# A decoder layer on one core: products of the high parts ahead of the low parts, a finer wait, and a new order on all five engines

## The reference, cut to what matters

```
h  = LN(x) * g + b, cut into 4 heads of 64
x1 = LN(x + (x + relu(h @ k.T)**2 @ v))         k, v = w_fc and w_proj.T as 1024 rows of 64, for all heads
Q, K, V = x1 @ Wq.T + bq, ctx @ Wk.T + bk, ctx @ Wv.T + bv                   (16 heads of 16)
D  = clip(frac_k - frac_q, -0.2, 0.2)
P  = softmax(gamma * Q @ K.T / 4 + delta * (alpha_pos * max(D, 0) + alpha_neg * min(D, 0)))
x2 = LN(x1 + (P @ V) @ Wo.T + bo)
e  = the largest of 8 of x2 @ gate_W.T + gate_b;   u = x2 @ lora_A[e].T       (rank 4)
f  = relu(x2 @ wi_W.T + wi_b + u @ lora_B[e].T)                               (1024 wide)
out = LN(x2 + f @ wo_W.T + wo_b)
```

## Time and profile before

| What | Value |
|---|---|
| median of 3 runs | 902.18 us (898.16 to 902.9) |
| the profiled execution's own time | 896.02 us |
| its span, from the first to the last instruction | 894.2 us |
| mean granted TensorE clock in it | 0.993 |
| TensorE busy, of the span | 839.8 us, 94% |
| VectorE, ScalarE, GpSimd busy | 760.4, 716.8, 587.9 us |

### The profile page before, as it was taken

The page is one execution under the profiler, slowest core; times in us unless marked ns, Lnnn a source line. Parts: engine busy times, 40 slices in busy tenths (PEclk is TensorE's granted clock), DMA queues, the critical chain, the costliest instruction groups (busy, mean ns, idle before and its releaser), DMA issues.

```text
span 894.2 us, 20601 instructions
## 1 busy us (share of the span) xinstructions
PE 839.8 (94%) x7012; PEld 667.6 (75%) x7012; DVE 760.4 (85%) x2158; ACT 716.8 (80%) x1949; POOL 587.9 (66%) x762
## 2 busy tenths in 40 slices
PE   2787989999999999999999999999999999999866
PEld 1354757878888787887877787788878787788766
DVE  4778889989898898989889898989889798899842
ACT  3568899888897988888897988889798888889821
POOL 2867776776767686776777586776768676544310
PEclk9999999999999999999999999999999999999998
DMA  6223323222132222223123222213222221313100
GB/s 173 86 51 55 65 38 62 38 46 41 43 67 58 43 49 54 43 56 58 43 42 72 37 43 54 54 43 50 64 42 48 50 49 24 77 22 53 31 12 23
DMA packets 40025, 46.12 MB, mean 52 GB/s; under 512 B 10257, under 2 KB 27153, under 8 KB 39922
## 3 DMA queue, kind: packets, MB, share of 16 engines
q1 hardware_dynamic: 39922, 44.82, 25.1%
HBM read 15.42 MB, written 4.19 MB: 22 GB/s over the span
## 4 chain that ended last, share of the span: by engine, by line
PE 87%; ACT 6%; DVE 3%; issue 2%; POOL 1%; POOLq 0%; DVEq 0%; ACTq 0%
PE bank L226 21%; PE bank L270 12%; PE bank L351 12%; PE bank L415 10%; PE bank L364 7%; PE bank L258 6%; PE bank L342 6%; PE bank L259 6%; ACT P L564 2%; PE bank L422 2%; PE bank L290 1%; ACT STG L489 1%; ACT R L510 1%; PE bank L376 1%; PE bank L247 1%
## 5 line engine op out<-in xcount | busy, mean ns | idle before, releaser
L988 POOL TENSOR_SCALAR U<-DP,alph 128x512 f32<-128x512 f32 x256 | 186.9, 731 | 128.4 <-DVE NM L778 72.6
L970 POOL TENSOR_TENSOR R<-R 128x512 f32<-128x512 f32 x212 | 228.0, 1076 | 64.2 <-ACT R L510 64.1
L564 ACT ACTIVATE P<-T,NM 128x256 f32<-128x256 f32 x512 | 256.3, 511 | 2.9 <-DVE NM L778 2.9
L771 DVE SCALAR_TENSOR_TENSOR bank<-DN,alph,bank 128x512 f32<-128x512 f32 x256 | 191.2, 747 | 40.8 <-PE bank L342 38.5
L778 DVE CUSTOM_DVE_ANT_0 T<-bank,U 128x256 f32<-128x256 f32 x512 | 197.0, 422 | 9.0 <-DVE bank L771 0.2
L510 ACT ACTIVATE R<-bank 128x512 f32<-128x512 f32 x256 | 152.6, 598 | 46.7 <-PE bank L259 42.3
L489 ACT ACTIVATE STG<-bank 128x512 f32<-128x512 f32 x256 | 152.4, 595 | 27.5 <-PE bank L351 25.7
L351 PE MATMUL bank<-ident,P 128*128 128x128 f32 x1024 | 155.5, 274 | 6.9 <-ACT STG L489 5.8
L351 PEld LDWEIGHTS bank<-ident,P 128*128 128x128 f32 x1024 | 117.5, 140 | 29.9 <-ACT P L564 14.7
L270 PE MATMUL bank<-R,VS 128*32 128x512 f32 x1024 | 124.1, 603 | 4.9 <-DVE R L727 3.9
L258 PE MATMUL bank<-SK,KH 128*128 128x512 f32 x256 | 115.5, 451 | 5.7 <-DVE SK L721 5.7
(11 more groups left out here) (164 smaller groups left out, 1887.7 us busy)
## 6 DMA issues: line engine op xcount, KB each, us to landing
QS<-QK SPq DMA_DIRECT2D x384, 64.0 KB, 2.3
XG<-in_x SPq DMA_DIRECT2D x16, 256.0 KB, 3.1
CT<-in_ctxT SPq DMA_DIRECT2D x16, 256.0 KB, 2.8
out<-XO SPq DMA_DIRECT2D x16, 256.0 KB, 2.5
FK<-in_frac SPq DMA_DIRECT2D x16, 128.0 KB, 3.2
STG<-in_wiT SPq DMA_DIRECT2D x2, 512.0 KB, 4.0
STG<-in_woT SPq DMA_DIRECT2D x2, 512.0 KB, 4.0
STG<-in_kT SPq DMA_DIRECT2D x2, 256.0 KB, 3.9
```

The lines of the kernel that those rows point to most:

```text
L564: eng.activation(P[n % NP][:, cs], T[n % NT][:, cs], ACT.Exp, bias=NM[:, n % 8, q:q + 1], scale=-1.0, accum_out=SU[n // 16 % 2][:, q, seat ...
L771: eng.scalar_tensor_tensor(out=L[:, :], in0=dn[:, :], scalar=alph[:, 16 + h:17 + h], in1=L[:, :], op0=ALU.mult, op1=ALU.add).then_inc(s_t1, 1)
L970: eng.tensor_tensor(r[:, :], r[:, :], r[:, :], ALU.mult).then_inc(s_sqp, 1)
L988: eng.tensor_scalar(U[n % NU][:, :], dp[:, :], alph[:, h:h + 1], 0.0, ALU.mult, ALU.add).then_inc(s_u, 1)
```

## The change

Four things. First, `kp`, `qp`, `vp`, `op` and `gate` run all products with the high part behind a wait for the high part alone, then wait for the low part and run its products. The number of matmuls stays the same (5986 instructions of that kind in both programs). Second, `ffn_out` waits per piece for the quarter that it reads. Third, the two low-rank matmuls become a step of their own, `low_rank`, with a place of its own in the order. Fourth, nearly all the numbers in `due` and the single instants are new on all engines, and with them the order.

```diff
             def kp(b):
...
-                pe.wait_ge(s_cl, b + 1)
+                pe.wait_ge(s_ch, b + 1)
                 wh, wl = W["k"]
                 for m in range(2):
                     cs = slice(m * 128, m * 128 + 128)
                     for k in range(2):
-                        mm3(bank[:, m * 256:m * 256 + 256], wh[:, k, cs], wl[:, k, cs], CH[:, k, :], CL[:, k, :],
-                            k == 0, k == 1, s_kp if m + k == 2 else None)
+                        for x in (wh, wl):
+                            eng.matmul(bank[:, m * 256:m * 256 + 256], x[:, k, cs], CH[:, k, :],
+                                       start=(m + k == 0 and x is wh), stop=False, skip_group_check=True)
+                pe.wait_ge(s_cl, b + 1)
+                for m in range(2):
+                    cs = slice(m * 128, m * 128 + 128)
+                    for k in range(2):
+                        i = eng.matmul(bank[:, m * 256:m * 256 + 256], wh[:, k, cs], CL[:, k, :], start=False,
+                                       stop=(k == 1), skip_group_check=True)
+                i.then_inc(s_kp, 1)
...
             def op(b):
-                pe.wait_ge(s_aol, b + 1)
-                by_tokens("op", b, "o", s_op)
+                by_tokens("op", b, "o", (s_aoh, b + 1), (s_aol, b + 1), s_op)
...
+
+            def low_rank(b, f2):
+                bank = bank_of["fi", b, f2]
                 pe.wait_ge(s_ull, b + 1)
...
-                    pe.wait_ge(s_il, 4 * b + 4)
                 bank = bank_of["fo", b, 0]
                 t = piece // 4
+                pe.wait_ge(s_il, 4 * b + piece % 4 + 1)
...
-                for b, u in due(g, 1327, 4, 22, early=-3, late=708):
+                for b, u in due(g, 1322, 4, 25, early=-1, late=761):
                     ffn_in(b, u)
-                for b, u in due(g, 1503, 8, 14, early=9, late=788):
+                for b, u in due(g, 1323, 4, 26, early=3, late=785):
+                    low_rank(b, u)
+                for b, u in due(g, 1467, 8, 19, early=13, late=779):
                     ffn_out(b, u)
-                for b, _ in due(g, 792):
+                for b, _ in due(g, 791, early=-43, late=-27):
                     rcT(b)
```

More of the change, by code:

```diff
@@ L314, in qp, with by_tokens @@
                     for k in range(2):
-                        mm3(bank[:, m * 256:m * 256 + 256], wh[:, k, cs], wl[:, k, cs], X1H[:, k, :], X1L[:, k, :],
-                            k == 0, k == 1, s_qp if m + k == 2 else None)
-            def by_tokens(name, b, w, done):
+                        for x in (wh, wl):
+                            eng.matmul(bank[:, m * 256:m * 256 + 256], x[:, k, cs], X1H[:, k, :],
+                                       start=(m + k == 0 and x is wh), stop=False, skip_group_check=True)
+                pe.wait_ge(s_x1l, b + 1)
+                for m in range(2):
+                    cs = slice(m * 128, m * 128 + 128)
+                    for k in range(2):
+                        i = eng.matmul(bank[:, m * 256:m * 256 + 256], wh[:, k, cs], X1L[:, k, :], start=False,
+                                       stop=(k == 1), skip_group_check=True)
+                i.then_inc(s_qp, 1)
+            def by_tokens(name, b, w, high, low, done):
                 bank, before = take(name, b)
@@ L321, in by_tokens @@
                 wh, wl = W[w]
+                pe.wait_ge(*high)
                 for t in range(2):
@@ L324, in by_tokens @@
                     for k in range(2):
-                        mm3(bank[:, t * 256:t * 256 + 256], CH[:, k, ts], CL[:, k, ts], wh[:, k, :], wl[:, k, :],
-                            k == 0, k == 1, done if t + k == 2 else None)
+                        for x in (wh, wl):
+                            eng.matmul(bank[:, t * 256:t * 256 + 256], CH[:, k, ts], x[:, k, :],
+                                       start=(t + k == 0 and x is wh), stop=False, skip_group_check=True)
+                pe.wait_ge(*low)
+                for t in range(2):
+                    ts = slice(t * 128, t * 128 + 128)
+                    for k in range(2):
+                        i = eng.matmul(bank[:, t * 256:t * 256 + 256], CL[:, k, ts], wh[:, k, :], start=False,
+                                       stop=(k == 1), skip_group_check=True)
+                i.then_inc(done, 1)
             def vp(b):
                 pe.wait_ge(s_wlo["v"], 1)
-                pe.wait_ge(s_cl, b + 1)
-                by_tokens("vp", b, "v", s_vp)
+                by_tokens("vp", b, "v", (s_ch, b + 1), (s_cl, b + 1), s_vp)
             def op(b):
-                pe.wait_ge(s_aol, b + 1)
-                by_tokens("op", b, "o", s_op)
+                by_tokens("op", b, "o", (s_aoh, b + 1), (s_aol, b + 1), s_op)
             def logits(n):
@@ L382, in gate @@
                 pe.wait_ge(s_wlo["g"], 1)
+                pe.wait_ge(s_x2h, b + 1)
+                o = bank[0:40, 0:256]
+                for k in range(2):
+                    for x in GA:
+                        eng.matmul(o, x[:, k, :], X2H[:, k, :], start=(k == 0 and x is GA[0]), stop=False,
+                                   skip_group_check=True)
                 pe.wait_ge(s_x2l, b + 1)
                 for k in range(2):
-                    mm3(bank[0:40, 0:256], GA[0][:, k, :], GA[1][:, k, :], X2H[:, k, :], X2L[:, k, :],
-                        k == 0, k == 1, s_gt if k == 1 else None)
+                    i = eng.matmul(o, GA[0][:, k, :], X2L[:, k, :], start=False, stop=(k == 1), skip_group_check=True)
+                i.then_inc(s_gt, 1)
             def gsT(b):
@@ L470, in _ @@
                     vp(b)
[L471 removed]
+                for b, _ in due(g, 1095, early=23, late=227):
                     turned_over("x2T", b, X2, s_x2, 2 * b + 2, s_x2T)
[L473 removed]
+                for b, _ in due(g, 1174, early=25, late=462):
                     gate(b)
[L475 removed]
+                for b, _ in due(g, 1245, early=-2, late=552):
@@ L630, in _ @@
                     rb(b)
-                for b, _ in due(g, 1065, early=4, late=146):
+                for b, _ in due(g, 1064, early=9, late=-39):
                     x2(b)
-                if g == -2184:
+                if g == -2226:
                     weight("v", W["v"][0][:, :, :], view(512, 1, 128, 2))
-                if g == -1698:
+                if g == -2006:
                     weight("k", W["k"][0][:, :, :], view(512, 2, 128, 2))
-                if g == -1144:
+                if g == -1184:
@@ L868, in _ @@
                     centred("a", b, XN, XG[b % 2], s_x0)
-                if g == -1537:
+                if g == -1593:
                     first_gain()
-                for b, _ in due(g, -1509, start=1, late=20):
+                for b, _ in due(g, -1504, start=1, late=56):
                     dve.wait_ge(d_x[b % 2], 16 * (b // 2 + 1))
                     stats("a", b, XG[b % 2])
-                for b, _ in due(g, 666):
+                for b, _ in due(g, 673, early=-2, late=-41):
                     rc(b)
-                for b, _ in due(g, 812):
+                for b, _ in due(g, 811, early=-31, late=32):
@@ L935, in _ @@
                     ull(b)
-                for b, u in due(g, -1133, 16, 37, early=-3, late=9):
+                for b, u in due(g, -1134, 16, 37, early=13, late=-32):
                     if on_dve(b, u):
@@ L1036, in _ @@
                     plus(X1b[b % 2], X1, boB, s_x1b)
-                for b, _ in due(g, 1396, early=123, late=634):
+                for b, _ in due(g, 1427, early=-161, late=883):
                     pool.wait_ge(s_x2, 2 * b + 2)
@@ L1041, in _ @@
                     plus(X2b, X2, woB, s_x2b)
-                for b, u in due(g, -1087, 16, 38, early=16, late=4):
+                for b, u in due(g, -1078, 16, 37, early=37, late=-33):
                     if not on_dve(b, u):
```

214 lines of the change are left out of this document (107 added, 107 removed).

## The result

The changed kernel takes 892.18 us (median of 4 runs, 887.95 to 892.82), the kernel before 901.73 us in runs beside them: a ratio of 0.9896, 95% interval 0.9858 to 0.9934. Forecast were 895 us and -7.1 us; measured are -9.5 us.

A forecast was written before the change was run, and what follows sets the result against it. TensorE was taken to bound the kernel, full in the steady blocks, so gains lie in start and end: 0 - 5.0 - 2.1 = -7.1 us, from 902.18 to 895 us; 8 in 10 range 888 to 904.

The forecast's parts named there:

- The steady part: 14 of the 16 blocks, TensorE always busy: no gain or cost, 0 us (-0.5 to +4.9).
- The tight 0.24 us: Steady blocks: slack between ScalarE's copy that frees a bank and `turn`, the tightest meeting found; expected to hold.
- The end: Kernel's end up to the last matmul: 3.4 us before the last feed-forward part plus 1.6 in it, -5.0 us (4.0 to 5.5).
- `op` (0.7) and `gate` (0.5): Kernel's end: high-part matmuls run before the low part is ready, taking about 0.7 and 0.5 us off the path.
- `x2T`: Kernel's end: no longer held behind eight pieces of `ffn_out`, it starts once x2 is there, 2.5 us sooner.
- The last part: Last feed-forward part: the 1.50 us wait for the last `IL` goes, perhaps 0.2 more; -1.6 us (-1.1 to -1.9).
- rival D: Last feed-forward part: two further quarters at 1.2 GHz cost 1.2 us each, leaving -4.7 us, 897.5; chance 0.07.
- The start: Kernel's start: 1.1 us from an earlier `restack` and another 1.1 later in the start; taken as -2.1 us (-3.5 to +1.0).
- the square: Start, on VectorE ahead of `restack`: a 1.55 us square fills a 0.51 us wait, winning 1.1 us (0.5 to 1.5).
- the prediction's own sign: Check in the profile after: if the last `values` comes later than before, the start's sum is wrong.
- the upper end of the range: Start: +1.0 us, block 0's `otT` coming later, twice the 0.5 us that one `scores` adds.
- the second half of the start: Later start: block 0's `ao` fills idle VectorE, `op` starts with the high part, `values` moves behind other pieces; 1.1 us.

The follow-up runs named there:

- before with fillers: The kernel before with 109 useless matmuls put into TensorE's idle time at start and end; 893.75 us, ratio 0.9925.
- after with fillers: The changed kernel with 97 useless matmuls in TensorE's idle time, 26 at the end and 71 in the start; 885.80 us, ratio 0.9821.

## Why the prediction was right, step by step

- **The steady part, 0: right.** A period is 51.31 us in both, measured over nine of them, and the split alone leaves M as it was. The tight 0.24 us held.
- **The middle outside it: missed.** My sum has no term for the stretch from 771 to 848, where VectorE is fuller than TensorE. M shrank by 1.1 us. The split alone gives none of it, the new order without the split none, and the new order with block 15's old instants a quarter. It needs both the split and the new order; which instruction comes earlier I did not isolate.
- **The end, -5.0 (4.0 to 5.5): right, and its terms too.** With the clock held in both it is -5.19. From `uT` of block 14 to that of block 15: predicted -3.4, measured -3.3 (25.98 to 22.65); the split's share is 1.2, as the sum had it for `op` (0.7) and `gate` (0.5) together, the order's 2.15. `x2T` gained 2.3 of the 2.5. The last part: predicted -1.6, measured -1.86 (14.55 to 12.69) with the clock held, but only -0.4 in the two profiles without fillers (15.51 to 15.11), since two quarters instead of one fell into 1.2 GHz. That is rival D, beside the forecast and not in its place: it cost the profiled execution 2.4 us of E, and the second profiled execution of before, at a clock of 0.984, loses more (44.42 against 40.70).
- **The start, -2.1: the size came out by luck, as two errors cancelled.** With the clock held S is -2.05, but neither term is what I had. I had the first `restack` 1.1 us earlier, because the square left the path. It came 3.1 us later, at 62.86, where the earlier trace rows has 59.80:

```profile
62.86 8.30 SPq L1121 DMA_DIRECT2D QS<-QK  x12
```

By the prediction's own sign (the last `values` later than before, 855.42 against 854.45, of which 0.5 us is `rcT`, now ahead of it) the start's sum is wrong. Only with the clock held do they come 2.8 us sooner. Even with fillers in both, `otT` of block 0 and the first `logits` start later. First before with fillers, then after with fillers:

```profile
44.02 0.60 PE L280 MATMUL bank<-ident,OT 128*128 128x128 f32 x4
...
63.86 0.39 PE L342 MATMUL bank<-QS 128*128 128x256 f32 x2
```

```profile
45.30 0.60 PE L280 MATMUL bank<-ident,OT 128*128 128x128 f32 x4
...
66.33 0.51 PE L365 MATMUL bank<-QS 128*128 128x256 f32 x2 [0.31 <-DMA QS<-QK]
```

In these two profiles `restack` is 2.2 us later (59.42 against 57.22), and three steps make it up. `otT` comes 1.3 us later; I had this only at the upper end of the range. From there to `x1T` it takes 0.9 us more: GpSimd's shift and scale for block 0, the row of 2.58 us, was held while VectorE ran four operations in a row. I had looked at VectorE's order and not at what its new order does to GpSimd. And from `x1T` to `restack`, where the square was to give 1.1 us, it gives nothing (6.33 against 6.32). The square's 1.55 us of the earlier trace rows are 0.68 with fillers, with the split alone and with the wait by quarters alone. I also misread: the row at 69.59 is the third `logits`, the first started at 66.16. What brought the time back is the second half of the start, from the first `logits` to block 0's `op`. I gave it 1.1 us; it won 1.9 in the two profiles without fillers (58.41 to 56.53) and 4.9 with them (59.52 to 54.62), where before has its low clock from 100 to 125 us. Which step wins this I did not isolate.
- **The remaining 1.6 us** of the 9.5 I put down to the clock and not to work: the forecast took the two kernels' executions for equal in clock and moved the median by the difference in one profile. Before sits mostly at 0.981 to 0.986, after at 0.989. The difference -9.5 + 7.95 = -1.6 us alone would not show it, as the interval of the -9.5 reaches from -5.9 to -12.8; the clocks do. The second profile of before has PEclk 0.50 from 861.5 to 864.5 us, right behind the idle 2.87 us ahead of `op`, and 0.86 from 100 to 125; both profiles of after have 1.00 at these places. That the shorter idle times of the new order are the reason was not tested by itself.

The Trainium skill ("TensorE: Matmul & The Clock Gate", "What's actually happening") says that the same kernel's number of matmuls at the lower clock varies from run to run; the 81 executions of before agree, with clocks from 0.981 to 0.993 and times from 895.2 to 904.1 us. The warning that I weighed, of small idle times between groups, fits the start and the end, where the clock fell, and not the stretch from 771 to 848, where PEclk stayed at 1.00 in every profile.

## What to carry to other kernels

Where one engine is full, look for the gain in the ramp and the drain, and read each chain there to its next late operand. Before trusting one profile's total, look at its mean clock beside that of the other runs: compare executions at an equal clock, or hold the clock with matmuls of no use in the waiting times and compare those. Check a sum term by term: here the start's total was right and its terms were not. When an engine's order is changed, look also at the engine that runs beside it.

## What the runs showed of the hardware

- Matmuls that nobody reads, put where TensorE waits, kept it at 2.4 GHz: 97 of them brought 892.70 down to 885.80 us, with 1.1 us between the fastest and the slowest of five executions. At the end they delayed nothing (22.64 us from `uT` to `uT` with and without them). In the start, TensorE at 1.2 GHz cost time although it had idle time beside: S fell by 4.2 us, from 175.87 to 171.66, when fillers held the clock there too.
- Two GpSimd operations on one number per partition took 2.58 us together instead of 0.51 while VectorE ran four operations with two inputs in a row. The second of them ended with VectorE's last, at 53.73 and 53.67 us. When VectorE waited for them, its last one started 0.18 us behind a GpSimd addition and took 2.31 us instead of 1.21. The row of VectorE in after:

```profile
52.46 1.21 DVE L718 TENSOR_TENSOR IL<-STG,IH 1x1024 fp32r<-1x1024 f32 x1
```

The Trainium skill ("SBUF — State Buffer", "Who interferes with whom") has the two engines share a pair of ports that one holds alone; the rows of 2.58 and 2.31 us agree.
